# Second attention: the maximum rows join the queries by a product with the identity, and ScalarE copies the results

## The reference, cut to what matters

```python
# x: [8, 256, 128]; 16 heads of 8 features
qkv = layernorm(x) @ qkv_w.T + qkv_b
q, k, v = split(qkv)                       # [8, 16, 256, 8] each
q = q * cos + rotate_half(q) * sin
k = k * cos + rotate_half(k) * sin
attn = softmax(einsum('abhqd,abhkd->abhqk', q, k) * 8 ** -0.5)
out = einsum('abhqk,bhkd->abhqd', attn, v)
x = x + out @ proj_w.T + proj_b
```

## Time and profile before

| what | value |
| --- | --- |
| median of 3 runs | 1136.32 us (1131.87 to 1139.19) |
| span of the profiled execution, first to last instruction | 1128.1 us |
| second attention, scores to last weighted sum | about 671 to 797 us |
| mean granted clock of PE | 0.859 |
| busy: PE, DVE, ACT, POOL | 86%, 87%, 62%, 31% |

### The profile page before, as it was taken

The page is one execution under the profiler, slowest core; times in us unless marked ns, Lnnn a source line. Parts: engine busy times, 40 slices in busy tenths (PEclk is TensorE's granted clock), DMA queues, the critical chain, the costliest instruction groups (busy, mean ns, idle before and its releaser), DMA issues. The chain is left out here.

```text
span 1128.1 us, 17423 instructions
## 1 busy us (share of the span) xinstructions
PE 974.6 (86%) x5403; PEld 708.3 (63%) x5403; DVE 982.1 (87%) x1491; ACT 695.7 (62%) x794; POOL 354.8 (31%) x214
## 2 busy tenths in 40 slices
PE   7746676766768999999999899999759999999997
PEld 5523343434446888888888645444647888888886
DVE  7798889888978999999999797996598999999997
ACT  4759999999975455544444562667444544444554
POOL 2036555655550334333332120100012333333430
PEclk9865555555558999999999998999969999999999
DMA  2000000000104855555551000000028655555531
GB/s 57 1 1 1 1 0 1 1 1 1 36 15 97 217 153 147 153 148 158 151 155 40 1 1 1 1 2 1 1 71 196 168 149 157 151 156 153 150 90 37
DMA packets 36478, 85.16 MB, mean 75 GB/s; under 512 B 5968, under 2 KB 19280, under 8 KB 36432
## 3 DMA queue, kind: packets, MB, share of 16 engines
q1 hardware_dynamic: 36432, 84.56, 28.2%
HBM read 82.45 MB, written 2.10 MB: 75 GB/s over the span
## 5 line engine op out<-in xcount | busy, mean ns | idle before, releaser
L1324 ACT ACTIVATE sg<-ps 128x512 f32<-128x512 f32 x264 | 156.8, 594 | 265.6 <-PE ps L473 264.1
L473 PE MATMUL ps<-xh,whi 128*128 128x512 f32 x528 | 206.6, 391 | 1.3 <-ACT b L1189 1.3
L473 PE MATMUL ps<-xh,wlo 128*128 128x512 f32 x528 | 206.3, 391 | 0.0
L473 PE MATMUL ps<-xl,whi 128*128 128x512 f32 x528 | 206.2, 391 | 0.0
L2070 DVE TENSOR_TENSOR hf<-sg,ps 128x512 f32<-128x512 f32 x264 | 170.3, 684 | 32.0 <-DVE hl L2077 24.4
L1471 POOL TENSOR_TENSOR rr<-xr,rr 128x2048 f32<-128x2048 f32 x32 | 144.9, 4548 | 163.5 <-ACT xr L1170 149.4
L1518 POOL CAST whi<-wraw 128x384 fp32r<-128x384 f32 x66 | 66.4, 1006 | 369.7 <-PE ps L473 321.5
L2077 DVE TENSOR_TENSOR hl<-hf,hh 128x1024 fp32r<-128x1024 f32 x132 | 179.1, 1357 | 0.5 <-DVE hf L2070 0.5
L2082 DVE TENSOR_TENSOR hf<-hf,cbc 128x1024 f32<-128x1024 f32 x128 | 157.5, 1231 | 13.3
L1372 ACT ACTIVATE hh<-hf 128x1024 fp32r<-128x1024 f32 x132 | 139.2, 1054 | 4.8 <-DVE hf L2082 4.8
L1520 POOL TENSOR_TENSOR wlo<-wraw,whi 128x384 fp32r<-128x384 f32 x66 | 117.4, 1778 | 5.3
(11 more groups left out here) (259 smaller groups left out, 1581.1 us busy)
## 6 DMA issues: line engine op xcount, KB each, us to landing
cbc<-routing_coefficients SPq DMA_DIRECT2D x256, 256.0 KB, 3.8
wraw<-in_wexp_dram SPq DMA_DIRECT2D x66, 192.0 KB, 2.8
X<-in_x_dram SPq DMA_DIRECT2D x4, 256.0 KB, 4.9
routing_coefficients<-cT SPq DMA_DIRECT2D x8, 128.0 KB, 2.3
out_dram<-X SPq DMA_DIRECT2D x4, 256.0 KB, 2.9
rope_in<-in_consts_dram SPq DMA_DIRECT2D x1, 512.0 KB, 3.5
wa<-in_wA_dram SPq DMA_DIRECT2D x1, 256.0 KB, 4.2
w_in<-in_wB_dram SPq DMA_DIRECT2D x1, 128.0 KB, 3.3
```

Source lines behind the costliest of these rows:

```text
L473: return pe.matmul(o, l, r, start=start, stop=stop, **kw)
L1324: act.activation(sg[c % 2][:, :], bank(4 + 2 * (c % 2)), ACT.Silu).then_inc(s_sg, 1)
```

## The change

- The sum of maximum rows and queries moves from DVE to PE. POOL makes `whole`, an identity matrix of 128x128, once. Behind each matmul of `mxT` with `mxs`, one of `whole` with the queries adds to the same 256 columns of PSUM. That is two more matmuls in each `b_max_selected`, 4 per sample, 32 in all.
- `max_rows` and what is left of `shift`, now the plain copy `shifted_queries`, move from DVE to ACT. They stand there behind the exponential of the step in which PE does the transpose or the product. Sample 0's three stand ahead of ACT's loop.
- DVE's loop keeps `head_max` and `max_split`.

```diff
             def b_max_selected(s, half):
 
+                if s == 0 and half == 0:
+                    pe.wait_ge(s_sel, 3)
                 if half == 0:
                     pe.wait_ge(s_mr, s + 1)
                 else:
                     pe.wait_ge(s_q2, 2 * s + 1)
                 for c in range(2):
-                    last = mm(bank(7)[:, c * N:(c + 1) * N], mxs[:, 2 * half + c, :], mxT[:, :])
+                    at = bank(7)[:, c * N:(c + 1) * N]
+                    mm(at, mxs[:, 2 * half + c, :], mxT[:, :], start=True, stop=False)
+                    last = mm(at, whole[:, :], b_qt[:, 2 * half + c, tok(s)], start=False, stop=True)
                 last.then_inc(s_mq, 1)
...
+                def max_rows(s):
+                    act.wait_ge(s_mT, s + 1)
+                    if s >= 1:
+                        act.wait_ge(s_mq, 2 * s)
+                    act.activation(mxT[:, :], bank(7)[:, 0:N], ACT.Copy).then_inc(s_mr, 1)
+
+                def shifted_queries(s, half):
+                    act.wait_ge(s_mq, 2 * s + half + 1)
+                    if s >= 2:
+                        act.wait_ge(s_s2, UNITS * (s - 1))
+                    act.activation(q2[s % 2][:, 2 * half:2 * half + 2, :], bank(7).rearrange("p (c n) -> p c n", c=2),
+                                   ACT.Copy).then_inc(s_q2, 1)
+
+                max_rows(0)
+                shifted_queries(0, 0)
+                shifted_queries(0, 1)
                 for U in range(B * UNITS + 3):
...
+                    s, at = (U + 3) // UNITS, (U + AHEAD) % UNITS
+                    if s < B and at == 0:
+                        max_rows(s)
+                    elif s < B and at in (1, 2):
+                        shifted_queries(s, at - 1)
...
+                pool.tensor_copy(whole[:, :], ident)
                 pool.tensor_copy(to_m, of_m).then_inc(s_sel, 1)
...
-                def max_rows(s):
-                    dve.wait_ge(s_mT, s + 1)
-                    if s >= 1:
-                        dve.wait_ge(s_mq, 2 * s)
-                    dve.tensor_copy(mxT[:, :], bank(7)[:, 0:N]).then_inc(s_mr, 1)
-
-                def shift(s, half):
-                    dve.wait_ge(s_mq, 2 * s + half + 1)
-                    if s >= 2:
-                        dve.wait_ge(s_s2, UNITS * (s - 1))
-                    cs = slice(2 * half, 2 * half + 2)
-                    dve.tensor_tensor(q2[s % 2][:, cs, :], bank(7).rearrange("p (c n) -> p c n", c=2),
-                                      b_qt[:, cs, tok(s)], ALU.add).then_inc(s_q2, 1)
...
-                for V in range((B + 1) * UNITS):
-                    if UNITS <= V < B * UNITS and V % UNITS == 0:
+                for V in range(B * UNITS):
+                    if UNITS <= V and V % UNITS == 0:
                         dve.wait_ge(s_ms, V // UNITS)
-                    if V < B * UNITS:
-                        head_max(V)
-                    s, at = V // UNITS - 1, V % UNITS
-                    if at == UNITS - 1 and V < B * UNITS:
-                        max_split(s + 1)
-                    elif at == 0 and s >= 0:
-                        max_rows(s)
-                    elif at in (1, 2) and s >= 0:
-                        shift(s, at - 1)
+                    head_max(V)
+                    if V % UNITS == UNITS - 1:
+                        max_split(V // UNITS)
```

More of the change, by code:

```diff
@@ L164, in hybrid @@
                 mxs = sb_("mxs", [P, CHUNKS, P], F32R)
+                whole = sb_("whole", [P, P], F32R)
                 with ExitStack() as pre_b:
```

## The result

The changed kernel takes 1136.51 us (median of 20 runs, 1133.39 to 1139.9). The ratio is 1.0033, interval 1.0023 to 1.0044: the change costs 3.8 us. The profiled execution has a span of 1137.3 us.

The account below looks back on a forecast made before the run. The prediction took the PE-DVE round trip of 1.38 us per step as the bound. Its terms, 0.86 + 0.86 + 2.25 + 0.7 = 4.7 us, added to the median of before gave 1141 us, range 1131 to 1148.

Parts of the forecast that it names:

- The rival of the cheap products: PE's products in second attention: 0.25 us per half instead of 0.43, sum 1.7 us, 1138 us; chance 0.17.
- The bound is the round trip of 1.38 us, not DVE's queue: Plain steps of second attention: scores, DVE's reduction and PE's rewriting of the bank set 1.38 us per step.
- the rival of the DVE bound: Second attention: DVE's queue sets the period, samples 2 to 6 gain 1.55 us each, 1131 us; chance 0.15.
- some 15 us of waiting for PE in all: DVE's reductions in second attention: waiting for PE in most steps, some 15 us in all instead of 12.
- Two more matmuls cost 0.43 us per half: PE's product in each half: two added matmuls at 0.215 us each, 0.86 per sample, 6.9 in all.
- The bound that I had drawn from the fillers' spacing: PE's added matmuls: with weight load hidden, 0.125 us each or 0.25 per half, from fillers 0.25 apart.
- A middle sample pays 0.45 us: Samples 2 to 6: delay left from the later products, 0.45 us each, 2.25 in all.
- The replay: Middle sample's steps 40 to 48 replayed with the new program: a delay of 0.41 to 0.47 us stays.
- Samples 0 and 1 pay 0.86 each: Products of samples 0 and 1 stand among fillers without a wait, so 0.86 us each is paid in full.
- The tail pays 0.7: Sample 7, without scores beside it: between 0.59 and 0.86 us, taken as 0.7, with ACT setting the pace afterwards.
- ACT's copies are covered, with a tenth to spare: Step 42, half 0: ACT's copy of shifted queries ready at 745.90, PE needs it by 746.02.
- Nothing outside the stage moves: Stages other than second attention are untouched, so nothing else can move except by being shifted.

Follow-up runs that it names:

- dve_light: Kernel before, with DVE's copy of the maxima and its two additions touching only 8 columns, nothing put on PE or ACT; ratio 1.0013.
- double: Changed kernel with one more product of `whole` and the queries before each product of the maxima, 32 matmuls more; ratio 1.0084.
- a_again: Changed kernel once more, unaltered, for a second profile; 1135.23 us, ratio 1.0032 to the kernel before.
- a_third: Changed kernel a third time, unaltered; 1135.02 us, ratio 1.0024 to the kernel before.
- act_light: Changed kernel, with ACT's copies of the maxima and of the shifted queries touching only 8 columns; ratio 1.0042 to the kernel before.
- null_whole: Kernel before plus only the new buffer and POOL's copy of the identity into it, which nobody reads; ratio 1.0001.
- trim: Changed kernel with six filler matmuls of 512 columns fewer in samples 0 and 1; ratio 1.0028 to the kernel before.
- b_hold: Kernel before with six matmuls of 512 columns filling PE's wait at the end of each expert phase; 1132.43 us, ratio 0.9994.
- a_hold: Changed kernel with the same six matmuls filling PE's wait at the end of each expert phase; 1133.48 us, ratio 1.0013.

## Why the prediction was right or wrong

The direction was right, and 1136.51 lies in the range and within 1% of before, as the chances had it. 1141 itself is 4.5 us too high, of which 3.6 are the three runs of before, which came out high. The change of +3.8 us looks like my +4.7, but it is not made of the terms that I added up: the stage holds 1.5 to 2.3 of it, and that the rest brings the sum so near to mine is luck. The rival of the cheap products had the stage right with 1.7, and it misses the whole by the same rest: 1134.4 from the 20 runs of before. By its steps:

- *The bound is the round trip of 1.38 us, not DVE's queue.* Right. dve_light takes away nearly all of DVE's moved work and gains 0.16 us per sample, where the rival of the DVE bound needed all of the 1.3 taken away. In the changed kernel plain steps still take 1.37 to 1.38, and DVE's wait moved up by 13 us, near the 12.4 that it lost; I had written some 15 us of waiting for PE in all, and it is 24.8, since work that leaves the queue without shortening the period comes back as waiting.
- *Two more matmuls cost 0.43 us per half.* Wrong, and this is the step that failed. They cost 0.24. I divided the time of a pair by two. The pair's 0.43 is 0.24 for its two matmuls and 0.19 that is paid once for the group, whatever its size; double shows 0.12 for each again. The bound that I had drawn from the fillers' spacing, 0.25 per half, was the true value, and I had put it into a rival with a chance of 0.17.
- *A middle sample pays 0.45 us.* Wrong by the same step: 0.07 to 0.08, which is 0.24 for the late products of half 1 less 0.17 that DVE gives back. The replay itself held. With 0.25 per half it gave 0.08, step 42 at 744.75, step 43 at 746.55 and step 44 at 747.92; after taking off 6.19 us, the rows give 744.75, 746.55 and 747.93. That rival's five samples, 0.4 us, are what the trace shows.
- *Samples 0 and 1 pay 0.86 each.* The first half of the stage, to sample 1's transpose, grew by 0.43 and 0.47 us in a_again and a_third and by 1.2 in the first profile, but kernels with the old stage show 17.4 to 18.2 us there themselves, so this term is measured only roughly. Sample 1 grew by 0.48 each time, which is PE's line with 0.24 per half. The mechanism (in line, without a wait) was right, the size was half.
- *The tail pays 0.7.* It pays 0.24 (15.46 against 15.22), and not through ACT.
- *ACT's copies are covered, with a tenth to spare.* Right. The copy was out at 751.84 for a product at 752.07, which with 0.12 for the signal is the tenth that I had reckoned, and act_light changes nothing.
- *Nothing outside the stage moves.* Not borne out. The stage accounts for 1.5 to 2.3 of the 3.0 to 4.35 us. With PE's clock held at the ends of the expert phases the two kernels lie 1.05 and 0.7 us apart. That points to those ends, but it is not proof: the ratios of the filled kernels to before are uncertain by some 2 us, and other stretches vary by 1.6 to 1.8 us from one profile to the next. All three profiles of the changed kernel had end 2 slow, and neither of the two of the kernel before; so had four of the seven others. Whether the change makes that fall likelier, by moving the moment of that end, or whether it was the draw, is open. End 1, ahead of the change, was slow in two of the three, too. What was shown is that no slow end was seen once the wait was filled, and that no excess beyond the stage's was measured then.

The prices put together, 0.45 + 0.48 + 0.4 + 0.24 = 1.6 us, agree with the stages of 113.5 in a_again and a_third against 112.0. The first profile's 114.3 has 0.8 more, all of it between the transposes of samples 0 and 1.

The Trainium skill, TensorE: Matmul & The Clock Gate, "Back-to-back issue gap", was weighed in the prediction with 131 ns per matmul for a sustained stream. That figure is for 512 columns, and the fillers with 512 columns need 0.25; but its claim that loads and matmuls overlap in a stream holds here, at 0.12 for 256 columns with a weight load each. The same page, "What's actually happening", says that the clock granted to PE depends on how busy it has been; ends 1 and 2, which fall after a wait and stay up once it is filled, agree.

## What to carry to other kernels

Price an added matmul by the distance between two starts inside a group of its own shape, never by a group's length over its count, since what is paid once for a group is then counted with every member (here 0.19 us of the 0.43 of a pair). Take load off an engine only after asking what a step waits for. Here DVE was busy for 48.41 of 52.55 us in four middle samples before (92%), still waited for its partner in most rounds, and taking 1.3 us of its work away gave back 0.16. Where a difference in time is larger than the stage's own, look for stretches with two lengths in the profiles, and hold them still before comparing.

## What the runs showed of the hardware

- PE needed 0.12 us for a matmul with 256 columns and a 128x128 weight load inside a group, and 0.19 us more for each group of such between matmuls on tiles of 32 rows or columns (0.43, 0.67, 0.91 for two, four and six).
- A copy out of PSUM of 128x512 took 0.60 us on ACT and 0.69 on DVE; of 128x8, 0.18 and 0.16.
- After an idle stretch of 1.96 us at full clock, PE's granted clock fell to half at 13 of 24 ends, from at once (null_whole, end 1) to about 1.3 us into the next work (trim, end 2), and at none of eight ends once six matmuls filled 1.5 us of the wait. A slow end costs 1.6 us, two of them 3.2 of the scatter of 9 us. With the waits filled twelve runs lay within 4.8 (b_hold) and 5.6 us (a_hold), and with six fillers less in samples 0 and 1 as well, within 2.4 and 3.3.
